# One square root for both first norms, and the second batch's rows moved behind the first keys

## The reference

```python
xn = layernorm(x)                      # (x - m) / sqrt(v + 1e-5)
# layer 0
h = xn * rsqrt(mean(xn * xn) + 1e-6) * norm_scale      # a second norm, of xn
s = xn + ssd(h @ in_proj_w) @ out_proj_w               # state space scan
g = silu(top2_of_8_experts(xn))
x = x + s * g
# layer 1
xn = layernorm(x)
s = attention(xn @ Wq.T, xn @ Wk.T, xn @ Wv.T) @ Wo.T  # rotated q and k, causal, 32 heads, 8 for k and v
a = sign(layernorm(xn) * gamma + beta)                 # again a norm of xn
g = silu((a @ sign(weight - mean).T + bias) * alpha)
x = x + s * g
```

## Time and profile before

| | us |
|---|---|
| median of 3 runs | 734.5 (734.28 to 734.57) |
| the profiled execution, its own time | 734.23 |
| span of its trace | 732.4 |
| TensorE busy | 686.1 (94%) |
| VectorE busy | 513.0 (70%) |
| ScalarE busy | 440.7 (60%) |
| GpSimd busy | 391.7 (53%) |

### The profile page before, as it was taken

One profiled execution on the slowest core, in us unless ns is written; L12 is line 12 of the kernel. 1 busy time (PEld: TensorE's weight loads), 2 busy tenths in 40 slices (PEclk: granted clock), 3 DMA queues, 4 the chain that ended last, 5 costly groups with the idle time before them and its releaser, 6 DMA issues.

```text
span 732.4 us, 13492 instructions
## 1 busy us (share of the span) xinstructions
PE 686.1 (94%) x4483; PEld 596.0 (81%) x4483; DVE 513.0 (70%) x1076; ACT 440.7 (60%) x1075; POOL 391.7 (53%) x442
## 2 busy tenths in 40 slices
PE   5999999999999999899889999999999999999995
PEld 3888999989999998687667888888788888787874
DVE  7584656434423335997888878888798878887775
ACT  4446344243331342567678788877877788878772
POOL 1314542423424232137566777877977788777550
PEclk9999999999999999999999999999999999999999
DMA  8158987787877746145442432334323423142011
GB/s 291 53 193 258 289 259 242 244 261 220 266 249 229 222 140 175 34 129 173 128 132 56 119 81 57 96 79 100 78 62 101 95 73 90 49 116 59 1 30 58
DMA packets 108453, 102.25 MB, mean 140 GB/s; under 512 B 51104, under 2 KB 78688, under 8 KB 108256
## 3 DMA queue, kind: packets, MB, share of 16 engines
q1 hardware_dynamic: 106272, 95.62, 45.2%
q0 software_dynamic: 2112, 5.77, 2.5%
HBM read 69.24 MB, written 11.14 MB: 110 GB/s over the span
## 4 chain that ended last, share of the span: by engine, by line
PE 63%; DVE 22%; ACT 7%; issue 5%; POOL 2%; DMA 1%; DVEq 0%; SPq 0%; ACTq 0%; POOLq 0%
PE bank L1735 14%; PE bank L1769 8%; PE bank L1570 6%; PE bank L1908 5%; DVE p_lo L1083 4%; PE bank L1875 3%; DVE nmax L1074 3%; DVE o_rest L1092 3%; PE bank L1574 3%; PE bank L1575 3%; PE bank L1576 3%; PE bank L1876 2%; DVE q_mix L1040 2%; DVE q_mix L1041 2%; ACT prob L1334 2%
## 5 line engine op out<-in xcount | busy, mean ns | idle before, releaser
L1532 POOL TENSOR_TENSOR prob<-prob,rinv 128x128 f32<-128x128 f32 (+3 forms) x256 | 176.4, 721 | 89.8 <-DVE rinv L1079 89.8
L1334 ACT ACTIVATE prob<-bank,nmax 128x512 f32<-128x512 f32 (+3 forms) x256 | 133.1, 525 | 41.1 <-DVE nmax L1074 32.8
L1083 DVE TENSOR_TENSOR p_lo<-bank,p_hi 128x512 fp32r<-128x512 f32 x160 | 109.2, 682 | 56.5 <-ACT p_hi L1341 54.4
L1341 ACT ACTIVATE p_hi<-bank 128x512 fp32r<-128x512 f32 x160 | 95.3, 595 | 42.3 <-PE bank L1570 41.4
L1735 PE MATMUL bank<-xgT,wm 128*128 128x128 f32 x920 | 111.3, 275 | 0.5 <-ACT xgT L1246 0.5
L1735 PEld LDWEIGHTS bank<-xgT,wm 128*128 128x128 f32 x920 | 108.7, 192 | 3.3 <-issue 1.4
L1875 PE MATMUL bank<-kT,qT 128*128 128x512 f32 (+3 forms) x256 | 83.6, 332 | 20.1 <-ACT prob L1334 15.7
L1570 PE MATMUL bank<-cst,prob 128*128 128x128 f32 x640 | 96.6, 274 | 1.4 <-POOL prob L1532 0.7
L1074 DVE TENSOR_REDUCE nmax<-bank 128x1 f32<-128x512 f32 (+2 forms) x192 | 91.0, 500 | 2.1 <-PE bank L1878 2.1
L1908 PE MATMUL bank<-p_lo,v_parts 128*128 128x256 f32 (+3 forms) x288 | 91.7, 341 | 0.2
L1505 POOL DMA_INDIRECT y_rows<-y_row,to_row x21 | 22.7, 1081 | 108.9 <-DVE y_row L943 86.4
(11 more groups left out here) (323 smaller groups left out, 1528.1 us busy)
## 6 DMA issues: line engine op xcount, KB each, us to landing
wm<-in_w_moe SPq DMA_DIRECT2D x23, 1280.0 KB
wm<-in_w_moe SPq DMA_DIRECT2D x23, 640.0 KB
qT<-q_hi SPq DMA_DIRECT2D x124, 64.0 KB, 2.0
qT<-q_lo SPq DMA_DIRECT2D x124, 64.0 KB, 2.0
wo_twice<-wo_hi SPq DMA_DIRECT2D x32, 128.0 KB, 2.5
k_exp<-k_rows SPq DMA_DIRECT2D x56, 64.0 KB, 2.0
wtl<-in_w_moe_tail SPq DMA_DIRECT2D x46, 64.0 KB
y_rows<-gate SPq DMA_DIRECT2D x1, 2048.0 KB, 14.0
```

Of the source, the lines that this page charges most:

```text
L1083: TT(p_lo[:, b_, :], bank[2 + b_ % 2][:, :], p_hi[:, b_, :].bitcast(F32), ALU.subtract).then_inc(plo_done, 1)
L1334: ins = actv(prob[:, i % 2, h, POFF[j]:POFF[j] + (j + 1) * P], bk[:, at:at + (j + 1) * P], ACT.Exp, bias=nmax[:, i % 2, h, j:j + 1], accum ...
L1341: actv(p_hi[:, b_, :], bank[2 + b_ % 2][:, :], ACT.Copy).then_inc(phi_done, 1)
L1532: ins = GT(seg, seg, rinv[:, i % 2, k, j:j + 1].to_broadcast([P, (j + 1) * P]), ALU.mult)
```

## The change

At the first norm, both arguments `v + 1e-5` and `v + 1e-6 * (v + 1e-5)` are written side by side, one square root on ScalarE takes both, and the reciprocal and the refining step work on both. `rrms` now holds the whole scale of `h`. The filler matmuls ahead of it go from five to three.

At the turn to the attention VectorE scales only tiles 0 to 3. GpSimd scales tiles 4 to 7, behind its split of the query weights. TensorE turns batch 1's parts (k = 2, 3) behind the first two key products, and VectorE makes their lower parts behind the first keys' rotation; the next norm's argument comes behind these. On ScalarE only the numbering of the roots changes, its list keeps its order: the copies for k = 2, 3, then the root, the exponential's table, and the value copies. The semaphore `pad_zero` is merged into `ones_ready`.

```diff
-            vec.memset(ptl[0:TAIL, :, :], 0.0).then_inc(pad_zero, 1)
+            vec.memset(ptl[0:TAIL, :, :], 0.0).then_inc(ones_ready, 1)
...
-            rsqrt(rstd, mv[:, :, 1], 1e-5)
-
-            then(TT(sv[:, 6, :], mv[:, :, 1], rstd, ALU.mult))
-            then(TT(sv[:, 6, :], sv[:, 6, :], rstd, ALU.mult))
-            rsqrt(rrms, sv[:, 6, :], 1e-6)
-            then(TT(sv[:, 7, :], rstd, rrms, ALU.mult))
-            for src, scale, ready in ((h_tok, sv[:, 7, :], h_ready), (xn_tok, rstd, xn_ready)):
+            both_args, both_roots, both_scales, both_more = (sv[:, 2 * i:2 * i + 2, :] for i in range(4))
+            then(TS(sv[:, 0, :], mv[:, :, 1], 1e-5, None, ALU.add))
+            TS(sv[:, 1, :], mv[:, :, 1], 1 + 1e-6, 1e-6 * 1e-5, ALU.mult, ALU.add).then_inc(var_ready, 1)
+            roots[0] += 1
+            dve.wait_ge(root_ready, roots[0])
+            then(vec.reciprocal(both_scales, both_roots))
+            then(TT(both_more, both_args, both_scales, ALU.mult))
+            then(TT(both_more, both_more, both_scales, ALU.mult))
+            then(TS(both_more, both_more, -0.5, 1.5, ALU.mult, ALU.add))
+            then(TT(both_scales, both_scales, both_more, ALU.mult))
+            for src, scale, ready in ((h_tok, rrms, h_ready), (xn_tok, rstd, xn_ready)):
...
-            for t in range(NT):
+            for t in range(TB):
                 TS(xn1[:, t, :], x_tok[:, t, :], mv[:, t, 0:1], rstd[:, t:t + 1], ALU.subtract, ALU.mult).then_inc(xn_ready, 1)
-            then(TT(sv[:, 6, :], mv[:, :, 1], rstd, ALU.mult))
-            then(TT(sv[:, 6, :], sv[:, 6, :], rstd, ALU.mult))
-            rsqrt_asked(sv[:, 6, :], 1e-5)
...
-            for k in range(KC * BATCH):
+            for k in range(KC):
                 lower_norm(k)
             for k in range(2):
                 rope_k(0, 0, k, bank[4 + k])
+            for k in range(KC, KC * BATCH):
+                lower_norm(k)
+            then(TT(sv[:, 6, :], mv[:, :, 1], rstd, ALU.mult))
+            then(TT(sv[:, 6, :], sv[:, 6, :], rstd, ALU.mult))
+            rsqrt_asked(sv[:, 6, :], 1e-5)
             for k in range(2):
                 rope_q(0, k)
...
-            root(0)
-            root(1)
+            act.wait_ge(var_ready, 1)
+            actv(sv[:, 2:4, :], sv[:, 0:2, :], ACT.Sqrt).then_inc(root_ready, 1)
...
             split_wq(0)
+            gp_.wait_ge(xn_ready, NT + TB)
+            for t in range(TB, NT):
+                gp_.tensor_scalar(xn1[:, t, :], x_tok[:, t, :], mv[:, t, 0:1], sv[:, 4, t:t + 1], op0=ALU.subtract,
+                                  op1=ALU.mult).then_inc(xn_later, 1)
...
-            keep_busy(bank[7][:, 0:3 * P], ident, cst[:, 0:3 * P], 5)
+            keep_busy(bank[7][:, 0:3 * P], ident, cst[:, 0:3 * P], 3)
...
-            for k in range(KC * BATCH):
+            for k in range(KC):
                 turn_norm(k, xn_ready, bank[k])
             pe.wait_ge(lo_done, KC * BATCH + 2)
             pe.wait_ge(w_lo_done, 4)
             pe.wait_ge(turns_ready, 2)
             for k in range(2):
                 make_k(0, 0, k, bank[4 + k])
+            for k in range(KC, KC * BATCH):
+                turn_norm(k, xn_ready, bank[k])
```

More of the change, by code:

```diff
@@ L444, in layered_kernel @@
         row_out = [sem(f"row_out{i}") for i in range(2)]
-        pad_zero, xg_full, xgT_ready, hid_full, sil_done, hE_done, row_full, row_taken = sems(
-            "pad_zero xg_full xgT_ready hid_full sil_done hE_done row_full row_taken")
-        mixed, gated = sems("mixed gated")
+        xg_full, xgT_ready, hid_full, sil_done, hE_done, row_full, row_taken = sems(
+            "xg_full xgT_ready hid_full sil_done hE_done row_full row_taken")
+        mixed, gated, xn_later = sems("mixed gated xn_later")
         sg_ready, back_full, x_ready, q_first, second_ready = sems("sg_ready back_full x_ready q_first second_ready")
@@ L891, in _ @@
             dve.wait_ge(pr_full, len(PROJS))
-            vec.memset(hE[0:TAIL, :, FULL * P:HC * P], 0.0).then_inc(pad_zero, 1)
+            vec.memset(hE[0:TAIL, :, FULL * P:HC * P], 0.0).then_inc(ones_ready, 1)
             def scan_front(c):
@@ L977, in _ @@
                     if n == 0:
-                        dve.wait_ge(pad_zero, 2)
+                        dve.wait_ge(ones_ready, 7)
                     dve.wait_ge(sil_done, 2 * n + 1)
@@ L1394, in _ @@
             ins.then_inc(turns_ready, 1)
-            root(2)
+            root(1)
             act.wait_ge(turns_full, 2)
@@ L1401, in _ @@
                 actv(xnT_hi[:, c, b * HALF:(b + 1) * HALF], bank[k][:, :], ACT.Copy).then_inc(hi_done, 1)
-            root(3)
+            root(2)
             actv(sv[:, 8, :], ones[:, 0:NT], ACT.Exp)
@@ L1667, in scan_decay @@
                 if c == 0:
-                    pe.wait_ge(ones_ready, 5)
+                    pe.wait_ge(ones_ready, 6)
                 pe.wait_ge(decay_ready, c + 1)
@@ L1763, in project @@
                 if j == 0:
-                    pe.wait_ge(pad_zero, 2)
+                    pe.wait_ge(ones_ready, 7)
                 pe.wait_ge(xgT_ready, min(j + 3, NJ))
@@ L1824, in turn_norm @@
                 b, c = k // KC, k % KC
-                pe.wait_ge(ready, (NT if ready is h_ready else NT) + (b + 1) * TB)
+                if ready is h_ready:
+                    pe.wait_ge(h_ready, NT + (b + 1) * TB)
+                elif b == 0:
+                    pe.wait_ge(xn_ready, NT + TB)
+                else:
+                    pe.wait_ge(xn_later, TB)
                 for t in range(TB):
```

## The result

The changed kernel takes 736.47 us (median of 12 executions, 734.69 to 737.46), the kernel before, run beside it, 734.52 us (12 executions, 734.28 to 735.52). The ratio is 1.0022, 95% interval [1.0015, 1.003]: slower by 0.22%, just over what can be told from no change. The forecast was 733.8 us with a range up to 735.6, so the time lies 0.9 us outside it. The profiled execution took 736.03 us with a span of 734.2 us, 1.8 us over the span of before.

The account below looks back on a forecast made before the run. TensorE bounds the kernel, busy 94% overall, so each seam counts by when its next long run starts. First seam -1.5 plus second +0.74 gives -0.76 us: 733.8 us from 734.5, range 732.6 to 735.6.

Parts of the forecast that it names:

- First seam: First norm: one root for both arguments lets the dt matmuls start earlier, 1.5 us won in sum.
- The 0.15 us for VectorE's late dt copy: Behind the dt matmuls: VectorE, ahead in its queue, takes their first result sooner, 0.15 us of 0.18 won.
- The removal of two fillers: Opening: three filler matmuls instead of five end near 10.5 us and hold nothing up; cover only.
- Keys 0.23 us earlier: Turn to the attention: less VectorE work ahead of the low parts, limited by ScalarE's copy; first key matmul at 307.13 us.
- Eight transposes on TensorE's path, +0.74 in all: Between keys and queries: moved transposes take 0.97 us, queries start 0.74 us later, passed in full to the end.
- Rival (a): Second seam costs nothing because the attention's first steps absorb the delay: 733.0 us, or 732.8; chance 0.18.
- GpSimd's scaling, 0.45 us each: Turn to the attention: four rows scaled by GpSimd, 0.45 us each, end near 306.2 us and cost 0.
- two products and the argument (0.6 together): VectorE behind the keys' rotation and two low parts: three small operations, 0.6 us, ahead of the first query rotation.
- GpSimd's addition of the keys: GpSimd's next work after its scalings: waits for rotated keys at 311.6 us and is not touched.
- rival (c): VectorE's line decides at the second seam, +1.3 us there: 734.3 us; chance 0.10.
- rival (d): TensorE's clock falls at the second seam or opening, matmuls at half rate, 2.0 us lost: 735.8 us; chance 0.14.
- the rule that transposes do not count for the clock: Second seam: by it the stretch is as empty before as after, so the clock's fall there drops away.

Follow-up runs that it names:

- number 7: Number 1 with five filler matmuls in the opening instead of three: 734.29 us, ratio 1.0001.
- Number 11: Number 5 with all eight rows scaled by VectorE and none by GpSimd: 733.88 us, ratio 0.999.
- number 5: Changed kernel with six filler matmuls ahead of the keys and the three small VectorE operations ahead of the keys' rotation: 734.07 us, ratio 0.9993.
- Number 3: Changed kernel with six filler matmuls in TensorE's gap behind the first eight transposes, ahead of the keys: 734.96 us, ratio 1.0008.
- Number 4: Changed kernel with the three small VectorE operations for the next root moved ahead of the keys' rotation: 735.54 us, ratio 1.0018.
- number 1: Changed kernel with the turn to the attention as before, so only the first norm's change: 734.09 us, ratio 0.999.
- number 9: Changed kernel with 25 instead of 19 filler matmuls ahead of the second norm's first transposes: 736.22 us, ratio 1.0016.
- number 10: Number 1 with 25 instead of 19 filler matmuls ahead of the second norm's first transposes: 733.09 us, ratio 0.9984.
- number 8: Changed kernel with GpSimd's four scalings in four operation forms, altering what three tiles compute: 736.06 us in one execution.

## Why the prediction was wrong

**First seam: right.** 1.37 us won and all of it carried to the second norm, held back by the weights' landing as worked out (`w_in_hi` at 10.32 us with that landing named as its release). The 0.15 us for VectorE's late dt copy didn't come: L1649 starts 1.36 us earlier than before (22.45 us), no more. The removal of two fillers was free, as costed; keeping them would have cost some 0.4 us (number 7).

**Keys 0.23 us earlier: nearly right.** They came at 4.24 us from the first row, 0.17 earlier than before, held back by ScalarE's copy as worked out. What the prediction didn't ask is which of the two things taken from VectorE won it. Number 11 has 4.24 with all eight scalings on VectorE: it is the three small operations (0.6 us) that had held the low part, not the four scalings (1.3 us).

**Eight transposes on TensorE's path, +0.74 in all: right.** In number 5 the transposes with the slower first query matmul take 0.89 us (0.97 in the sum), less the 0.17 of the keys. Numbers 5 and 11 have the first maximum at 22.83, 0.71 later than before (22.9 forecast), and their times are 0.55 and 0.51 us below before, where the sum said 0.76 with the 0.15 that didn't come. Rival (a), that the attention absorbs it, falls.

**GpSimd's scaling, 0.45 us each: mis-sized,** outside its own bounds of 0.38 and 0.77. It measured 1.21, and stayed hidden: the last ended at 307.90 us, and TensorE asked for them behind the keys, at 310.1 (at about 308.7 with the clock held). The room of 5.6 us that the prediction had worked out for the four is what made the error harmless.

**First failed step: "two products and the argument (0.6 together)".** They took 1.65 us (from 312.72 to the rotation at 314.37), since the place they were moved to lies beside GpSimd's addition of the rotated keys, which before ran beside VectorE's rotations alone. The same kind of stall stood in the trace of before, 1.95 us for a 128x32 operation while GpSimd split the output weights in the opening, and the prediction didn't look for it:

```profile
23.70 1.95 DVE L765 TENSOR_TENSOR dts<-dtB,par 128x32 f32<-128x32 f32 x1
...
23.23 2.37 POOL L1442 TENSOR_TENSOR w_out_lo<-w_out_sb,w_out_hi 128x1024 fp32r<-128x1024 f32 x1 [0.23 <-ACT w_out_hi L1183]
```

The prediction wrote that GpSimd's addition of the keys "is not touched"; it didn't ask what that addition does to the operations moved beside it. With the stall VectorE's line decides: the sum of the queries comes at 15.37 us from the first row, and ScalarE waits for it for 0.89 us. Number 3 has it without the clock: upper queries at 15.20 against 14.2. Number 4 moves the three away from the addition, and it is gone. That is rival (c)'s place, priced at +0.5 over the forecast where it is +1.0. The Trainium skill (GPSIMD Engine Reference, section 1, Specifications) says that GpSimd shares its SBUF interfaces with VectorE, with contention when a VectorE instruction has two SBUF inputs or runs in a two-port mode. The trace agrees on the first: L1138, with both inputs in SBUF, took 1.21 us, and the query rotations of the kernel before, with one input in a bank, 0.68 to 0.69 beside the same addition. L707, with one tensor as input, was slowed too (0.45 us, number 5); in which mode it ran, no run shows.

**Second failed step: rival (d), the clock's fall, left out of the sum and weighed at 0.14.** The mechanism (idle 1.62, transposes, idle 1.7, matmuls at half rate) was described as it happened, and priced at 2.0 where it is 1.44 us. Its weight was wrong: ten of twelve executions of the change were longer. Two arguments had lowered it: that the level held through the idle 1.62 us before, and the rule that transposes do not count for the clock, by which the stretch is as empty before as after. Against the first, number 1 shows the clock falling with TensorE's order unchanged, so one profile in which it held was no evidence of a margin. Against the use of the second: by it the change even shortened the stretch that counts as empty, from 4.50 us (302.86 to 307.36) to 4.33 (301.49 to 305.82), and yet the longer executions, at whichever place, went from 23 of 111 to ten of twelve. And number 9 has 3.04 us without another matmul, eight transposes and then 1.64 us idle, and seven of eleven executions are the longer; number 10 has 3.21 us, 2.29 of them sixteen transposes, and two of eleven are. A stretch of transposes and one that is half idle don't go the same way here. The Trainium skill (TensorE: Matmul & The Clock Gate, Part 4: PE-mode transpose) says of a transpose only that "it doesn't count as PE-busy the same way", which is less than the prediction took from it; it can be right of transposes alone, but it doesn't carry the conclusion that was drawn from it.

**The sum.** -1.37 + 0.74 + 1.0 (stall) + 1.44 (clock) = +1.8 us: 736.3 by the median of before, measured 736.47. Either term alone would have left the time inside the range (about 734.9 or 735.3, with 735.6 its top); the prediction took its rivals one at a time and had no sum for two at once. They are independent: number 3 and number 4 each took one away and left the other.

**Open:** why the clock falls in some executions of one program and holds in others; why six of eleven executions of number 1 are longer and only 23 of before's 111, with the same order of work at the turn 1.4 us later, and at which place; why the lower level lasted so much longer in four executions of number 4; and the spread of number 7.

## What to carry to other kernels

When a change opens or lengthens an idle stretch of TensorE ahead of a run of wide matmuls, look at the times of single executions and the mean granted clock of each, not at one profile. Here groups 1 to 1.5 us apart were, with the exception in number 7, executions with a lower mean clock, and six filler matmuls that ended before the awaited operand came cut the longer ones from ten of twelve to two of eleven (number 3) and none of eleven (number 5). Before moving even a 0.17 us operation on VectorE, look at what GpSimd does at the new place. And before moving work off an engine, ask what the next operation on it waits for: VectorE's 1.3 us were not on the path, so handing them to GpSimd won nothing. And an estimate taken from a row must be of the same operation, not only of the same engine and width.

## What the hardware showed that was not expected

- GpSimd's `tensor_scalar` on 128x256 fp32 takes 1.21 to 1.23 us with `subtract` first and a multiplication behind it (1.13 with a constant factor), and 0.55 us with `add` and `mult` in either order (number 8).
- A VectorE product of 128x8 elements with both inputs in SBUF took 1.21 us beside GpSimd's addition of two 128x512 tiles, against 0.17 alone. The addition of a constant to 128x8 elements took 0.45 us beside GpSimd's `tensor_scalar` (number 5) and 0.17 with GpSimd idle at the same place (number 11).
- The same program, on one chip, held TensorE's clock in some executions and not in others: in number 1 five of eleven have a mean granted clock of 0.999 or 1.000 and six 0.997. Of the changed kernel 2 of 12 were at 734.7 to 734.9 us, 7 at 736.0 to 736.7 and 3 at 737.1 to 737.5, with means of 0.998, 0.996 to 0.997 and 0.995. The steps fit a fall at the turn (1.4) and one at the last projection on top (some 1.0; it was 1.3 in number 11); only the first is in its profile.
